# A decoder layer on one core: where ScalarE's tables are loaded, two norms on GpSimd, and another order

## The chip, the cores and the metric

The kernel runs on one core of a Trainium2 chip. The metric is the device time of one execution in microseconds. A core has five engines that run their own instruction streams and meet at semaphores: TensorE (PE in the profile; PEld is its weight load), VectorE (DVE), ScalarE (ACT), GpSimd (POOL) and SyncE (SP), which here only issues DMAs. Products land in PSUM, which TensorE writes and VectorE and ScalarE read; GpSimd works on SBUF alone.

## What is computed

One post-norm decoder layer in float32, for x of shape (4, 1024, 256) and a context of shape (4, 77, 256):

```python
# block 1: sigmoid attention within the rows
q, k, v = x @ Wq.T + bq, x @ Wk.T + bk, x @ Wv.T + bv
qn, kn = layer_norm(q), layer_norm(k)                 # over the 256 columns
attn = sigmoid(qn @ kn.T / sqrt(256) - log(1024))
x = layernorm(x + (attn @ v @ Wo.T + bo) * layerscale)          # the first norm
# block 2: softmax attention over the 77 context rows, 16 heads of 16
qh, kh, vh = heads(x @ wq.T + bq), heads(ctx @ wk.T + bk), heads(ctx @ wv.T + bv)
x = layernorm(x + merge(softmax(qh @ kh.T / 4) @ vh) @ dense.T + b)   # the second norm
# block 3: a channel mix with the row before (zero ahead of row 0)
xr, xk = mu_r * x + (1 - mu_r) * x_prev, mu_k * x + (1 - mu_k) * x_prev
r, kk = sigmoid(xr @ W_r.T), square(relu(xk @ W_k.T))
x = layernorm(x + r * (kk @ W_v.T))                             # the third norm
```

Every norm is (x - mean) / sqrt(var + 1e-5) over the columns.

## The kernel before

The 4096 rows are 32 tiles of 128 rows, taken as 16 pairs (`NJ`). Four pairs are one batch. Products run as three float32r products of a high and a low part each (`split_product`, line 281); so each factor is first copied rounded by ScalarE (`..._hi`, the `copy` of line 460) and its rest taken by VectorE or GpSimd (`..._lo`, line 1170 on VectorE).

Block 1, for pair i: `qk` (query and key product) and their norms, `tqk` (transposes), `v`, then four `scores(4i..4i+3)`, each a 128x512 bank `st` that ScalarE turns into `a_sb` by `sigmoid` (line 510) and copies by `sigmoid_hi`, and four `attend` into the bank `acc`. `attended` and `stats1` on VectorE, `deviation1` on GpSimd (lines 908 to 913, scale `rsl` and bias `nbl`), and `norm1` on ScalarE, which writes x*rsl + nbl back into the rows `xs`.

Block 2: `x1` (transposes of the normed rows, line 1739), `query`, and for each tile t `cross_scores` (line 1886) into four banks `xb`, `maxima` on VectorE (line 1275, four groups of heads, each releases one group of exponentials), `exponentials(t, n)` on ScalarE (line 550, four groups of four 128x77 ACTIVATEs), `fold_weights` (line 948) and `normalise` (line 953) on GpSimd with `sums` and `reciprocals` on VectorE between them, `weights_t` (transposes, line 1899), `mixed` (line 1915), `dense`, and the second norm, on ScalarE for the first seven pairs and on GpSimd after them (line 972, x*rs + nb). The transposes use the same four banks as the logits, so `x1(i)` waits for all exponentials of tile 2i-1, `weights_t(t)` for those of tile t+1, and `cross_scores(t)` for those of tile t-1 and for the copies of the transposes of tile t-2.

Block 3: `x2` (transposes), `carried` (ScalarE, line 460), `halo` (GpSimd, line 984), `mixes` (VectorE, line 1340), `mix_hi`, `mix_lo`, `receptance`, `mix_keys`, `mix_values`, `gate_sigmoid`, `key_relu`, `key_squares`, `gated` (VectorE, line 1364, writes `y`), `residual3` (GpSimd, line 990, adds the rows), `stats3` (VectorE), `deviation3` (GpSimd, lines 997 to 1005) and `norm3`: pairs 0 to 10 on GpSimd (line 1011), 11 to 14 on ScalarE, 15 on VectorE.

Each engine's order is written out by hand: a list of calls for the start, a loop `round_(r)` of calls `at(call, index, count, first)` for the middle, a list for the late part, and `mix_round(i)` and a list for the tail. An engine works strictly in that order. Waits are `w.wait_ge(*sem)`; one that an earlier wait of the engine already covers is left out. ScalarE holds one set of function tables at a time; Sigmoid and Exp are in different sets, while Identity, Relu and Square don't make it load. Nobody writes the loads: where the next ACTIVATE needs the other set, the program gets an ACT_TABLE_LOAD in front of it. If that ACTIVATE has one wait, the wait stays on the ACTIVATE; if it has two, one of them stands on the load.

## Time and profile before

| | us |
|---|---|
| median of 3 runs | 562.71 |
| lowest, highest | 561.57, 563.49 |
| the profiled execution | 561.43 |
| its span | 559.6 |

The span begins with the first instruction on an engine and ends with the last; 1.8 us of the execution lie around it. Roughly, the start lasts until 85 us, the middle rounds until 336 us, the late part of blocks 1 and 2 (no projections left, block 3 beginning from 409 us) until 476 us, and the tail is block 3 alone. The rest is read as follows. A busy share says how much of a stretch an engine spent on instructions, waiting not included. The waits name for each engine which engine's instruction ended an idle time last. The chain goes back from the last instruction to what released it, and so on, so that only its parts set the end.

### The profile page before, as it was taken

What the parts mean: (1) busy time and instruction counts of PE and PEld (TensorE: products, weight loads), DVE (VectorE), ACT (ScalarE), POOL (GpSimd) and SP (SyncE); (2) the same over time, 40 slices, a digit from 0 to 9 for tenths busy, and PEclk for the clock granted to TensorE, in tenths of its full rate; (3) what the DMA queues carried; (4) which work ended last, traced back from release to release, by engine and by line L of the source; (5) the groups of instructions that cost most, each with busy time, mean ns of one, the idle gap of its engine ahead of it and who ended that gap; (6) DMA issues with size and microseconds to landing.
All of it is one profiled execution on the core that took longest, in us unless ns stands there. A gap on an engine that the chain in (4) does not pass through costs nothing.

```text
span 559.6 us, 12593 instructions
## 1 busy us (share of the span) xinstructions
PE 517.6 (92%) x4526; PEld 469.0 (84%) x4526; DVE 450.5 (80%) x1000; ACT 453.9 (81%) x1081; POOL 386.8 (69%) x514
## 2 busy tenths in 40 slices
PE   6989999999999999999999999998996968999873
PEld 4878988898989898998989898877885757999873
DVE  4677859779888788888888887677877998989975
ACT  3672569889899999998899899978897879878854
POOL 2773556766685959586868668466754567799996
PEclk9999999999999999999999999999999999999998
DMA  6511021010001011010101011214100000011113
GB/s 177 164 45 57 2 57 43 2 39 1 2 2 57 1 57 32 27 57 2 58 1 39 2 39 39 68 30 149 41 8 32 1 1 1 20 40 39 57 45 107
DMA packets 24400, 23.01 MB, mean 41 GB/s; under 512 B 2346, under 2 KB 24338, under 8 KB 24338
## 3 DMA queue, kind: packets, MB, share of 16 engines
q1 hardware_dynamic: 24050, 21.94, 12.9%
q8 instruction: 36, 0.59, 0.5%
q10 hardware_dynamic: 288, 0.26, 0.2%
q14 instruction: 26, 0.21, 0.1%
HBM read 15.07 MB, written 6.82 MB: 39 GB/s over the span
## 4 chain that ended last, share of the span: by engine, by line
PE 60%; ACT 14%; DVE 12%; POOL 8%; issue 4%; DMA 1%; POOLq 0%; SPq 0%; DVEq 0%; ACTq 0%
PE st L281 14%; PE acc L281 12%; PE proj L281 9%; PE xb L281 8%; ACT p_sb L550 6%; PE xb L1899 5%; PE xb L1915 4%; PE xb L1886 4%; POOL y L1011 3%; ACT L550 3%; DVE xm L1340 3%; DVE xmT_lo L1170 2%; PE proj L1797 2%; POOL y L990 2%; PE xb L1739 1%
## 5 line engine op out<-in xcount | busy, mean ns | idle before, releaser
L550 ACT ACTIVATE p_sb<-xb,neg_mx 128x77 f32<-128x77 f32 x512 | 118.6, 375 | 1.3 <-DVE neg_mx L1275 1.0
L953 POOL TENSOR_TENSOR p_sb<-p_sb,rc 128x1280 f32<-128x1280 f32 x32 | 78.2, 2443 | 38.6 <-DVE rc L1288 38.6
L948 POOL TENSOR_TENSOR fold<-p_sb 128x640 f32<-128x640 f32 x32 | 50.8, 1587 | 46.6 <-ACT p_sb L550 46.6
L281 PE MATMUL st<-qkT_hi 128*128 128x256 f32 x256 | 76.8, 300 | 0.0
L281 PE MATMUL acc<-vv_hi,aT_hi 128*128 128x256 f32 x256 | 75.5, 295 | 0.5 <-DVE aT_lo L1170 0.5
L281 PE MATMUL st<-qkT_lo,qkT_hi 128*128 128x256 f32 x256 | 72.4, 283 | 0.0
L281 PE MATMUL acc<-vv_hi,aT_lo 128*128 128x256 f32 x256 | 72.3, 283 | 0.0
L281 PE MATMUL acc<-vv_lo,aT_hi 128*128 128x256 f32 x256 | 72.3, 282 | 0.0
L281 PE MATMUL st<-qkT_hi,qkT_lo 128*128 128x256 f32 x256 | 72.3, 282 | 0.0
L1275 DVE TENSOR_REDUCE neg_mx<-xb 128x4 f32<-128x308 f32 x128 | 54.8, 468 | 13.9 <-PE xb L1886 13.6
L1295 DVE COPY pT<-xb 128x512 f32<-128x512 f32 x64 | 43.8, 685 | 19.6 <-PE xb L1899 19.0
L510 ACT ACTIVATE a_sb<-st,nlogs 128x512 f32<-128x512 f32 x64 | 44.0, 689 | 16.6 <-PE st L281 12.0
L281 PEld LDWEIGHTS st<-qkT_hi 128*128 128x128 f32 x256 | 48.7, 190 | 9.1 <-issue 8.6
L1899 PE MATMUL xb<-ident,p_sb 128*128 128x128 f32 x320 | 49.2, 275 | 7.5 <-ACT p_sb L550 6.3
L281 PEld LDWEIGHTS acc<-vv_hi,aT_hi 128*128 128x128 f32 x256 | 48.9, 191 | 1.4 <-DVE aT_lo L1170 0.9
L1170 DVE TENSOR_TENSOR aT_lo<-a_sb,aT_hi 128x512 fp32r<-128x512 f32 x64 | 48.5, 761 | 1.2 <-ACT aT_hi L460 1.2
L897 POOL TENSOR_TENSOR vv_lo<-v_sb,vv_hi 128x512 fp32r<-128x512 f32 x16 | 20.6, 1289 | 41.3 <-ACT vv_hi L460 41.3
L281 PEld LDWEIGHTS st<-qkT_lo,qkT_hi 128*128 128x128 f32 x256 | 48.9, 191 | 0.1
L281 PEld LDWEIGHTS acc<-vv_lo,aT_hi 128*128 128x128 f32 x256 | 48.9, 191 | 0.1
L550 ACT ACT_TABLE_LOAD x30 | 38.5, 1283 | 12.9 <-DVE neg_mx L1275 12.5
L281 PEld LDWEIGHTS st<-qkT_hi,qkT_lo 128*128 128x128 f32 x256 | 48.9, 191 | 0.0
L281 PEld LDWEIGHTS acc<-vv_hi,aT_lo 128*128 128x128 f32 x256 | 48.8, 191 | 0.0
(232 smaller groups left out, 1764.5 us busy)
## 6 DMA issues: line engine op xcount, KB each, us to landing
xraw<-in_xT SPq DMA_DIRECT2D x16, 256.0 KB, 2.9
xs<-in_x SPq DMA_DIRECT2D x16, 256.0 KB, 2.7
out_y<-y SPq DMA_DIRECT2D x16, 256.0 KB, 2.1
x_kept<-xs SPq DMA_DIRECT2D x10, 256.0 KB, 2.1
x2s_a<-x_kept SPq DMA_DIRECT2D x2, 512.0 KB, 5.3
x2s_b<-x_kept SPq DMA_DIRECT2D x2, 512.0 KB, 7.8
x2s_c<-x_kept SPq DMA_DIRECT2D x1, 512.0 KB, 3.6
cT<-in_cT SPq DMA_DIRECT2D x1, 308.0 KB, 3.1
```

The costliest lines, as they stand in the source:

```text
L281: mm = pe.matmul(out, s_, m_, start=first and k == 0 and q == 0, stop=last and k == n - 1 and q == 2, skip_group_check=not check)
L510: act.activation(a_sb[:, i % NAR], st_bank[i % 2], ACT.Sigmoid, bias=nlogs[:, 0:1], scale=1.0 / 16).then_inc(sg_act.sem, 1)
L550: ex = act.activation(weights(t)[:, h // KH * (H // 2) + KH * n + h % KH, 0:SC], logits[n][:, h * SC:(h + 1) * SC], ACT.Exp, bias=neg_mx[: ...
L897: pool.tensor_tensor(lo, tiles(v_sb[:]), f(hi), ALU.subtract).then_inc(v_pool.sem, 1)
L948: pool.tensor_tensor(fold[:].rearrange("p (h k) -> p h k", k=FO), p[:, :, 0:FO], p[:, :, FO:2 * FO], ALU.add).then_inc(fo_pool.sem, 1)
L953: pool.tensor_tensor(weights(t), weights(t), rc[:, t % 2].rearrange("p (h o) -> p h o", o=1) .to_broadcast([P, H, SP]), ALU.mult).then_inc ...
L1170: return dve.tensor_tensor(lo, whole, f(hi), ALU.subtract)
L1275: dve.tensor_reduce(neg_mx[:, t % 2, HG * n:HG * (n + 1)], logits[n][:, 0:HG * SC].rearrange("p (h k) -> p h k", k=SC), AX, ALU.min)\
L1295: dve.tensor_copy(pT[:, 4 * c:4 * c + 4, (t % 2) * P:(t % 2 + 1) * P], tiles(tp_bank(c), 4))\
L1886: mm = pe.matmul(logits[n][:, e * KW:(e + 1) * KW], xq[own, e * D + u * P:e * D + (u + 1) * P], kb[own, b, e], start=True, stop=True)
L1899: mm = pe.transpose(tp_bank(c)[:, (n - 4 * c) * P:(n - 4 * c + 1) * P], p_sb[:, t % NP, n * P:(n + 1) * P], ident[:])
L1915: mm = pe.matmul(pv_bank[32 * n:32 * (n + 1), k * D:(k + 1) * D], vb[:, n, half, :, :, KC * b + k].rearrange("p a d -> p (a d)"), pT[:, 5 ...
```

## The change

ScalarE: `table_for(func)` is called at the head of `sigmoid`, `exponentials` and `gate_sigmoid`. Where the function differs from that of the call before, it issues an ACTIVATE of `func` on one column (`nlogs`, 128x1) into a column of `spare` that nobody reads, and the table load goes in front of that one. There are 61 such ACTIVATEs, and 62 loads before and after.

GpSimd: the first norm of pairs 11 to 15 (`N1 = 11`) is done there as multiply and add; `x1` and `deviation1` wait for the engine that does it. The third norm of pairs 0 to 10, still on GpSimd, becomes x*rs3 + nb3 in place of (x - mean)*rs3; so `nb3` is computed for all pairs but the last, and `stats3` waits for `nb3` of the pair two before it instead of for its norm.

The order of all engines is written anew. The rounds on ScalarE and TensorE start one pair later with more written out ahead of them; what a round does is the same but for its order.

```diff
+N1 = 11
+NSPARE = 8
...
+        def self_norm(i):
+            return ln1_act.at(i) if i < N1 else ln1_pool.at(i - N1)
...
+                loaded, spares = [None], count()
+                def table_for(func):
+                    if loaded[0] != func:
+                        loaded[0] = func
+                        w.wait_ge(*consts_pool.at(0))
+                        n = 8 * (next(spares) % NSPARE)
+                        act.activation(spare[:, n:n + 1], nlogs[:], func)
                 def sigmoid(i):
+                    table_for(ACT.Sigmoid)
                     w.wait_ge(*st_pe.at(i))
...
                 def exponentials(t, n):
+                    table_for(ACT.Exp)
                     w.wait_ge(*pads_pool.at(0))
...
                 def gate_sigmoid(i):
+                    table_for(ACT.Sigmoid)
                     w.wait_ge(*fr_pe.at(i))
...
                 def round_(r):
-                    at(exponentials, 2 * r - 6, NT, 2, 2)
-                    at(tqk_hi, 2 * r + 5, NT, 13)
+                    at(xt_hi, r + 3, NJ, 9)
+                    at(weights_tail, 2 * r - 9, NTA, 3)
...
                 def deviation1(i):
                     w.wait_ge(*ln1s_dve.at(i))
                     if i:
-                        w.wait_ge(*ln1_act.at(i - 1))
+                        w.wait_ge(*self_norm(i - 1))
...
+                def norm1(i):
+                    w.wait_ge(*ln1n_pool.at(i))
+                    for t in range(2):
+                        x1 = rows_of(i)[:, t]
+                        pool.tensor_scalar(x1, x1, rsl[:, t:t + 1], nbl[:, t:t + 1], ALU.mult, ALU.add).then_inc(ln1_pool.sem, 1)
...
                 def deviation3(i):
                     w.wait_ge(*fvs_dve.at(i))
                     if i - 2 >= NJ - NL:
                         w.wait_ge(*ln3_act.at(i - 2 - (NJ - NL)))
+                    elif i >= 2:
+                        w.wait_ge(*ln3_pool.at(i - 2))
...
-                    if NJ - NL <= i < NJ - 1:
-                        n, nb = i - (NJ - NL), nb3[:, i % 2]
+                    if i < NJ - 1:
+                        nb = nb3[:, i % 2]
...
                 def norm3(i):
-                    w.wait_ge(*ln3s_pool.at(i))
+                    w.wait_ge(*ln3n_pool.at(i))
                     for t in range(2):
                         yt = y[:, i % NY, t]
-                        pool.tensor_scalar(yt, yt, mv3[:, i % 2, t, 0:1], rs3[:, i % 2, t:t + 1],
-                                           ALU.subtract, ALU.mult).then_inc(ln3_pool.sem, 1)
+                        pool.tensor_scalar(yt, yt, rs3[:, i % 2, t:t + 1], nb3[:, i % 2, t:t + 1],
+                                           ALU.mult, ALU.add).then_inc(ln3_pool.sem, 1)
...
                 def stats3(i):
-                    if i - 2 >= NJ - NL:
-                        w.wait_ge(*ln3n_pool.at(i - 2 - (NJ - NL)))
-                    elif i >= 2:
-                        w.wait_ge(*ln3_pool.at(i - 2))
+                    if i >= 2:
+                        w.wait_ge(*ln3n_pool.at(i - 2))
...
                 def x1(i):
-                    w.wait_ge(*ln1_act.at(i))
+                    w.wait_ge(*self_norm(i))
```

How the order moves at the places that matter later. First ScalarE in late attention, from the sigmoid ahead of the exponentials of tile 27 to the transposed rows of pair 14. `p_sb<-xb` is an exponential, `a_sb<-st` a sigmoid, `xs<-xs,nbl,rsl` the first norm, `x1T_hi` the copy of the transposed rows. Before:

```order
L510 ACTIVATE a_sb<-st,nlogs 128x512 [waits s_st_dve,s_st_pe]
L550 ACT_TABLE_LOAD [waits s_mx_dve]
L550 ACTIVATE p_sb<-xb,neg_mx 128x77 [waits s_tp_pe]
L550 ACTIVATE p_sb<-xb,neg_mx 128x77 x3
...
L460 ACTIVATE xs<-xs,nbl,rsl 128x256 [waits s_ln1n_pool]
L460 ACTIVATE xs<-xs,nbl,rsl 128x256
L460 ACTIVATE aT_hi<-a_sb 128x512 [waits s_av_pe,s_sg_act]
L460 ACTIVATE x1T_hi<-xb 128x512 [waits s_tx_pe]
```

And now the same tile and pair:

```order
L521 ACT_TABLE_LOAD
L521 ACTIVATE spare<-nlogs 128x1
L570 ACTIVATE p_sb<-xb,neg_mx 128x77 [waits s_mx_dve,s_tp_pe]
L570 ACTIVATE p_sb<-xb,neg_mx 128x77 x3
...
L521 ACT_TABLE_LOAD
L521 ACTIVATE spare<-nlogs 128x1
L529 ACTIVATE a_sb<-st,nlogs 128x512 [waits s_st_dve,s_st_pe]
L468 ACTIVATE x1T_hi<-xb 128x512 [waits s_tx_pe]
```

The wait for the maxima (`s_mx_dve`) has left the load, the first norm has left ScalarE, and a sigmoid with its load stands ahead of the transposed rows.

Second GpSimd, in the tail, around the last residual add with the second batch's rows (`x2s_b`) and the first with the third's (`x2s_c`); `rs3` and `nb3` are scale and bias of the third norm, `y` its rows. Before:

```order
L1011 TENSOR_SCALAR y<-y,mv3,rs3 128x256
L990 TENSOR_TENSOR y<-y,x2s_b 128x512 [waits s_fva_dve]
L997 TENSOR_TENSOR rs3<-mv3,consts 128x2 [waits s_fvs_dve]
L999 TENSOR_TENSOR rs3<-rs3,consts 128x2 [waits s_ln3s_pool]
L984 COPY carry<-carry 128x4 [waits s_ca_act,s_xm_dve]
L990 TENSOR_TENSOR y<-y,x2s_c 128x512 [waits s_fva_dve]
```

And now:

```order
L1067 TENSOR_TENSOR rs3<-mv3,consts 128x2 [waits s_ln3_pool,s_fvs_dve]
L1069 TENSOR_TENSOR rs3<-rs3,consts 128x2 [waits s_ln3s_pool]
L1072 TENSOR_TENSOR nb3<-mv3,consts 128x2
L1075 TENSOR_TENSOR nb3<-nb3,rs3 128x2 [waits s_ln3n_pool,s_ln3s_pool]
L1058 TENSOR_TENSOR y<-y,x2s_b 128x512 [waits s_fva_dve]
L1052 COPY carry<-carry 128x4 [waits s_ca_act,s_xm_dve]
L1058 TENSOR_TENSOR y<-y,x2s_c 128x512 [waits s_fva_dve]
L1081 TENSOR_SCALAR y<-y,rs3,nb3 128x256 [waits s_ln3n_pool]
L1081 TENSOR_SCALAR y<-y,rs3,nb3 128x256
```

Each pair has two small instructions more, and the norm reads `rs3` and `nb3` in place of `mv3` and `rs3`.

## Rows read from the trace of the kernel before

**Rows 1.** The page: busy us and shares; TensorE's busy tenths in 40 slices

```profile
PE 517.6 (92%) x4526; PEld 469.0 (84%) x4526; DVE 450.5 (80%) x1000; ACT 453.9 (81%) x1081; POOL 386.8 (69%) x514
...
PE   6989999999999999999999999998996968999873
```

**Rows 2.** Stretches: length, busy us and instructions of each engine, clock, DMA share, GB/s

```profile
200.00:226.07 26.07, 26.07 (x242) 23.90 (x241) 21.91 (x50) 23.69 (x60) 18.99 (x25) 1.00 0.11 32
...
336.00:434.00 98.00, 88.51 (x834) 78.00 (x833) 72.14 (x149) 83.19 (x213) 60.72 (x67) 1.00 0.17 52
434.00:476.00 42.00, 33.99 (x326) 29.15 (x325) 38.67 (x84) 36.95 (x103) 27.39 (x35) 1.00 0.01 1
490.00:546.00 56.00, 48.98 (x396) 47.16 (x394) 49.27 (x117) 42.80 (x90) 54.90 (x66) 1.00 0.14 48
```

**Rows 3.** TensorE in order of time: start us, us, what; one middle round

```profile
199.93 0.28 PE L281 MATMUL xb<-x1T_hi,wx_hi 128*128 128x256 f32 x1
...
209.57 0.47 PE L281 MATMUL proj<-wqk_hi,xT_hi 128*128 128x512 f32 x1
209.88 0.40 PE L281 MATMUL proj<-wqk_lo,xT_hi 128*128 128x512 f32 x1
210.11 0.39 PE L281 MATMUL proj<-wqk_hi,xT_lo 128*128 128x512 f32 x1
...
226.00 0.28 PE L281 MATMUL xb<-x1T_hi,wx_hi 128*128 128x256 f32 x1
```

**Rows 4.** Waits, 336:476 and 476:560: who for whom, us, times, longest

```profile
ACT L550 <- DVE neg_mx L1275: 10.6, 8, 3.3
...
DVE st L1374 <- POOL y L990: 6.0, 6, 1.4
```

**Rows 5.** Groups of ScalarE, whole span: busy us, mean ns, idle before

```profile
L550 ACT ACTIVATE p_sb<-xb,neg_mx 128x77 f32<-128x77 f32 x512 | 118.6, 375 | 1.3 <-DVE neg_mx L1275 1.0
...
L550 ACT ACT_TABLE_LOAD x30 | 38.5, 1283 | 12.9 <-DVE neg_mx L1275 12.5
L510 ACT ACT_TABLE_LOAD x29 | 37.2, 1283 | 0.5
```

**Rows 6.** ScalarE in order of time; in brackets idle before, and releaser

```profile
76.12 1.28 ACT L550 ACT_TABLE_LOAD   x1 [1.92 <-DVE neg_mx L1275]
...
405.71 1.28 ACT L550 ACT_TABLE_LOAD   x1 [0.85 <-DVE neg_mx L1275]
...
407.01 3.57 ACT L550 ACTIVATE p_sb<-xb,neg_mx 128x77 f32<-128x77 f32 x16
...
430.73 1.28 ACT L550 ACT_TABLE_LOAD   x1 [3.33 <-DVE neg_mx L1275]
```

**Rows 7.** The chain that ended last: start us, us, what; tile 27, pair 14

```profile
416.82 1.28 ACT L550
...
421.68 0.98 ACT xs L460 x2
...
422.71 0.67 PE xb L1739 x4
```

**Rows 8.** GpSimd in order of time: start us, us, what

```profile
418.09 0.20 POOL L913 TENSOR_TENSOR nbl<-nbl,rsl 128x2 f32<-128x2 f32 x1
...
504.44 1.10 POOL L972 TENSOR_SCALAR xs<-xs,rs,nb 128x256 f32<-128x256 f32 x2
505.52 2.43 POOL L1011 TENSOR_SCALAR y<-y,mv,rs 128x256 f32<-128x256 f32 x2
```

**Rows 9.** Groups of GpSimd, whole span: busy us, mean ns, idle before

```profile
L1011 POOL TENSOR_SCALAR y<-y,mv,rs 128x256 f32<-128x256 f32 x22 | 28.3, 1294 | 0.2
...
L972 POOL TENSOR_SCALAR xs<-xs,rs,nb 128x256 f32<-128x256 f32 x18 | 12.6, 709 | 0.1
...
L1002 POOL TENSOR_TENSOR nb<-mv,consts 128x2 f32<-128x2 f32 x4 | 0.9, 232 | 0.0
L1005 POOL TENSOR_TENSOR nb<-nb,rs 128x2 f32<-128x2 f32 x4 | 0.8, 198 | 0.6
```

More of the change, by code:

```diff
@@ L1 @@
 from contextlib import ExitStack
+from itertools import count
 import numpy as np
@@ new lines, in round_ @@
+                    at(weights_tail, 2 * r - 9, NTA, 3)
+                    at(sigmoid, 4 * r - 7, NS, 16)
+                    at(mixed_hi, r - 5, NJ, 1)
+                    at(sigmoid, 4 * r - 6, NS, 16)
+                    at(exponentials, 2 * r - 7, NT, 4, 0)
+                    at(exponentials, 2 * r - 7, NT, 4, 1)
+                    at(exponentials, 2 * r - 7, NT, 4, 2)
+                    at(sigmoid_hi, 4 * r - 7, NS, 16)
+                    at(exponentials, 2 * r - 7, NT, 4, 3)
@@ new lines, in round_ @@
+                    at(norm1, r - 3, N1, 3)
+                    at(sigmoid_hi, 4 * r - 6, NS, 16)
+                    at(tqk_hi, 2 * r + 4, NT, 15)
+                    at(x1_hi, r - 3, NJ, 3)
+                    at(sigmoid, 4 * r - 5, NS, 16)
+                    at(v_hi, r + 2, NJ, 7)
+                    at(norm2, r - 6, N2)
+                    at(weights_tail, 2 * r - 8, NTA, 3)
+                    at(sigmoid, 4 * r - 4, NS, 16)
+                    at(query, r - 3, NJ, 2)
+                    at(sigmoid_hi, 4 * r - 5, NS, 16)
@@ L733, in _ @@
                 weights_tail(0)
+                query(1)
+                sigmoid(12)
+                exponentials(2, 0)
+                exponentials(2, 1)
                 sigmoid_hi(11)
+                exponentials(2, 2)
+                tqk_hi(13)
+                exponentials(2, 3)
+                weights_tail(1)
+                sigmoid(13)
+                sigmoid_hi(12)
+                mixed_hi(0)
+                sigmoid(14)
+                exponentials(3, 0)
+                exponentials(3, 1)
+                exponentials(3, 2)
+                exponentials(3, 3)
+                sigmoid_hi(13)
+                norm1(2)
+                xt_hi(8)
+                tqk_hi(14)
+                sigmoid_hi(14)
+                x1_hi(2)
+                sigmoid(15)
+                sigmoid_hi(15)
+                weights_tail(2)
                 for r in range(NJ):
                     round_(r)
+                sigmoid(57)
+                mixed_hi(11)
+                sigmoid_hi(57)
+                exponentials(25, 0)
+                exponentials(25, 1)
+                exponentials(25, 2)
+                exponentials(25, 3)
+                sigmoid(58)
+                x1_hi(13)
+                sigmoid_hi(58)
+                sigmoid(59)
+                sigmoid(60)
+                query(13)
+                exponentials(26, 0)
+                sigmoid_hi(59)
+                exponentials(26, 1)
+                sigmoid_hi(60)
                 exponentials(26, 2)
                 exponentials(26, 3)
-                carried(0)
                 sigmoid(61)
@@ L742, in _ @@
                 sigmoid_hi(61)
-                sigmoid(62)
                 exponentials(27, 0)
@@ L747, in _ @@
                 exponentials(27, 3)
-                norm1(14)
+                sigmoid(62)
+                x1_hi(14)
                 sigmoid_hi(62)
-                x1_hi(14)
+                carried(0)
                 sigmoid(63)
+                query(14)
                 sigmoid_hi(63)
-                query(14)
                 exponentials(28, 0)
@@ L1575, in _ @@
                 maxima(4, 2)
+                sigmoid_lo(15)
+                sigmoid_lo(16)
+                weights_body(3, 0)
                 for r in range(NJ):
```

649 lines of the change are left out of this document (333 added, 316 removed).

## Prediction

> **What bounds the kernel now.** I read the busy shares first, then the same shares by stretch, then in each stretch the wait that ends last. The page says TensorE 92%, ScalarE and VectorE 80 to 81%, GpSimd 69% [rows 1]. The 40 slices of 14 us show that these shares are an average over stretches that differ: TensorE has a 9 in every slice from 42 to 378 us, 6 to 9 in the seven after them, and 8, 7 and 3 in the last three [rows 1].
>
> *Middle rounds.* One whole round (a pair of row tiles) takes 26.07 us: the query product starts at 199.93 and again at 226.00 [rows 3]. In it TensorE is busy for all of the 26.07 us with 242 matmuls, ScalarE for 23.69, GpSimd for 18.99 [rows 2]. Nothing that shortens ScalarE or GpSimd shortens such a round. ScalarE has 2.38 us of idle time in it.
>
> *Late attention, 336 to 434 us.* No projections are left to fill TensorE: it is busy for 88.51 of 98 us, and its weight loads for 78.00, where the share of the middle rounds (23.90 of 26.07) would give 89.8 [rows 2]. So 9.5 to 12 us of TensorE's time are lost here. The chain of waits says to whom: maxima on VectorE, a table load of 1.28 us on ScalarE, 16 exponentials, the first norm (0.98 us), and only then TensorE's transposes [rows 7]. The row of waits says that ScalarE sat idle 10.6 us in 8 places before a table load of the exponentials [rows 4].
>
> *Tail, 490 to 546 us.* Only the third block is left. GpSimd is busy 54.90 of 56 us, VectorE 49.27, TensorE 48.98, ScalarE 42.80 [rows 2]. VectorE waited 6.0 us of it for GpSimd's residual add [rows 4]. GpSimd bounds this stretch, with VectorE 6.7 us behind.
>
> **The change, part by part.**
>
> *Table loads ahead of waits.* The number of loads stays 62. In the order of before, the first exponential of a tile from 20 on has two waits, and the one on the maxima stands on the load; in the changed order it stands on the exponential, with a 128x1 ACTIVATE between. Sigmoid loads gain nothing: all 29 together waited 0.5 us [rows 5]. Exponential loads of the middle rounds did not wait either; their 12.9 us of idle time is in nine places [rows 5], eight of them in late attention. There the load can now run inside the idle time, so each place gains the smaller of its wait and 1.28 us, less what the ACTIVATE adds where the wait is short. The eight waits sum to 10.6 us [rows 4]; the longest, 3.33 [rows 6], is cut to 1.28, which leaves 8.5.
>
> Price of the new ACTIVATE: no row shows a 128x1 on ScalarE. The nearest is the 128x77 exponential: 16 take 3.57 us, 223 ns apart [rows 6]. Not below nothing, since it does the engine no service; not above 375 ns, the mean of a 77-column one by itself [rows 5]. I take 0.17 us, below the spacing because it has 76 columns less. The seven shorter waits are about as long as the load or shorter, so 7 x 0.17 = 1.2 is lost there: 8.5 - 1.2 = 7.3 us, between 5.9 (at 0.375 us) and 8.5. All eight places are on the chain, as [rows 7] shows for one. In the middle rounds four of them cost 0.7 us (1.5 at most) and lie in ScalarE's 2.38 us of idle time; without that cover they would cost their full price on each of some ten rounds.
>
> The skill (Trainium skill, "ScalarE: Activation LUTs", section "What ACT_TABLE_LOAD costs") puts a switch at 1283 ns plus a drain of about 1380. The load agrees; the drain does not show, as the exponentials at 407.01 begin 1.30 us after the start of their load [rows 6]. With a drain on each of the eight places the gain by that page would be up to twice as large where the wait is long enough; I leave it out.
>
> *First norm of pairs 11 to 15 on GpSimd.* ScalarE loses ten ACTIVATEs, GpSimd gains ten instructions of the shape of its second norm, 0.55 us each when undisturbed (1.10 for two), 0.71 in the mean [rows 8, 9]. On the chain the ScalarE norm of pair 14 starts at 421.68, after the exponentials, though GpSimd had its numbers at 418.29 [rows 7, 8]. GpSimd would be done by 419.4, before the exponentials end, so 0.98 us leaves the chain. The same stands at pairs 12 and 13 (374.24 and 397.91, not repeated): 3 x 0.98 = 2.9 us. But the new order puts a sigmoid and its load where the norm was (1.28 + 0.17 + 0.69 = 2.1 us), ahead of the copy of the transposed rows, which before began 1.7 us after the exponentials; so that copy comes 0.4 us later and all behind the two of them 1.0 us earlier. I take 2.0 us, between -1 and 4. What is queued behind it on GpSimd is the second norm's numbers and the next fold; GpSimd is busy 60.72 of 98 us here [rows 2], which covers 5.5 to 7.1 us more.
>
> *Sum for late attention.* 7.3 + 2.0 = 9.3 us, against 9.5 to 12 us that TensorE loses there. A chain hardly gives back all of its length, because the next one (VectorE's, seen as the wait of 3.33 us, which is VectorE working through its own queue) is close behind. I take three quarters: -7.0, between -3 and -10.
>
> *Third norm as multiply and add.* GpSimd's (y - mean) x rs takes 1294 ns per tile, its x rs + nb of the same shape 709 [rows 9]; undisturbed neighbours in the tail are 1.10 us for two at 504.44 and 2.43 for two at 505.52 [rows 8]. 22 tiles x 0.585 = 12.9 us saved. Eleven more pairs need nb, 0.232 + 0.198 us each [rows 9] = 4.7 us. Net -8.2 us of GpSimd, on the engine that bounds the tail. But VectorE comes next after 6.7 us, and ScalarE's and TensorE's queues are near too. I take -5, between -2 and -7. The last few us behind the last product keep their length: pairs 11 to 14 stay normed on ScalarE and 15 on VectorE.
>
> Here a page speaks against the change. By the Trainium skill, "GPSIMD Engine Reference", section 3.1, GpSimd's time goes by the number of tensor inputs, two being the dear case. Both forms have one, so by that page only the 4.7 us of nb would be left and the edit would cost time. Rows decide: at the same shape, in the same stretch, 1.10 against 2.43.
>
> *New order.* On TensorE a middle round has the same 242 matmuls, but four runs of transposes instead of three. A product that follows such a run starts its second matmul after 0.31 us instead of 0.23 [rows 3], so about 0.1 us per round: +1.0 over ten rounds. For the explicit part I have no price, only that neighbours are exchanged and nothing moves by more than a few places: 0, between -3 and +3. Start: the first exponential load sat behind 1.92 us of waiting at 76.12 [rows 6] on the chain; -1.28 and three ACTIVATEs of 0.17 us, about -0.8, between 0 and -2.
>
> **Sum.** -7.0 - 5 + 1.0 - 0.8 = -11.8 us. The profiled execution took 561.43 us (span 559.6), so 549.6. The median of the runs shown is 1.28 us higher, so I forecast 550.9 us.
>
> **The rivals.**
>
> *A. The gains are eaten.* VectorE is busy 38.67 of 42 us in 434 to 476 [rows 2], the stretch that takes over what late attention gives back. If what late attention saves waits again there and VectorE takes half of the tail's gain, -3.5 - 2.5 + 1 - 0.8 = -5.8: 557 us. For it: the wait of 3.33 us. Against it: VectorE's 72.14 of 98 us before that.
>
> *B. Slower: ScalarE becomes the bound of the middle rounds.* Place: the four loads of a round, each with an ACTIVATE more. It decides from the point where the ACTIVATE costs over 0.6 us (2.38 / 4), or where the new order leaves ScalarE's idle time in places that it cannot use, so that each round grows by the full four. Price at 0.375 us: 1.5 us x 10 rounds = +15, with -11.8 for the rest: +3.2, 566 us. Against it: 91% busy with idle time spread over four waits in a round.
>
> *C. The form doesn't matter.* If GpSimd's norm was slow for its place and not for its operations, the saturated tail gets 4.7 us longer: -7.0 + 4.7 + 1.0 - 0.8 = -2.1, 560.6 us. Against it stands the pair of rows above.
>
> *D. More than the sum.* The chain gives back all (-9.3), the tail its 6.7, the order another 3, the start 0.8: -19.8, 543 us.
>
> **How the numbers follow.** Forecast (545 to 554) 0.55; A 0.20; B 0.08; C 0.04; D 0.08; 0.05 for something unseen, half of it on either side. The range reaches from D's edge to just beyond A: 543 to 560. A measurement of this kernel can tell about 0.3%, 1.7 us. Faster: forecast, A, D and most of C and the unseen, 0.87; same 0.04; slower 0.09.
>
> **What would show it.** Table loads before exponentials with no wait on maxima, and waits on the exponential itself; the first norm of pairs 12 to 14 gone from the chain; the third norm on GpSimd near 0.6 to 0.7 us; GpSimd under 90% from 490 us on with VectorE above; a middle round of 26.1 to 26.2 us. A round above 26.5 us is B; a third norm of 1.2 us is C; late attention as long as before with other waits is A.

## The result, and the profile after

The changed kernel takes 540.09 us in the median (539.50 to 540.18), the kernel before, beside it on the same chip, 562.14 (561.37 to 563.49). The ratio is 0.9603, with a 95% interval of 0.9581 to 0.9625: 22.05 us less, where 11.8 less were forecast and 543 was the low end of the range. The direction was right, the size was not. In the profiled executions the span went from 559.6 to 538.4 us, 21.2 less.

The page of the changed kernel answers [rows 1]: busy us, share, instructions, and TensorE's and VectorE's busy tenths in 40 slices.

```profile
PE 513.4 (95%) x4526; PEld 467.9 (87%) x4526; DVE 448.4 (83%) x1000; ACT 452.9 (84%) x1132; POOL 374.1 (69%) x546
...
PE   6999999999999999999999999999999987999994
...
DVE  4786878888888888887979797778878989999995
```

TensorE now has a 9 in every slice from 13 to 525 us but two, which lie from 431 to 458 us. The stretches of [rows 2], a round of 25.97 us first:

```profile
199.70:225.67 25.97, 25.97 (x243) 23.81 (x242) 22.10 (x50) 23.88 (x63) 17.80 (x24) 1.00 0.11 32
336.00:434.00 98.00, 94.46 (x925) 84.39 (x924) 79.43 (x175) 87.62 (x245) 69.93 (x83) 1.00 0.16 51
434.00:476.00 42.00, 37.51 (x347) 33.24 (x348) 40.07 (x90) 39.28 (x98) 32.29 (x48) 1.00 0.03 9
490.00:546.00 56.00, 40.48 (x332) 39.60 (x331) 41.52 (x105) 38.07 (x79) 40.29 (x74) 0.95 0.17 58
```

In late attention TensorE works 94.46 us of 98, against 88.51. In the middle rounds it is full, as before. In the tail GpSimd is busy for 40.29 us behind 490, less than VectorE's 41.52, as the prediction's sign had it; the kernel ends at 538.4.

The groups by line answer [rows 5, 9]: busy us, mean ns, idle before.

```profile
L521 ACT ACT_TABLE_LOAD x61 | 78.3, 1283 | 1.1
L1081 POOL TENSOR_SCALAR y<-y,rs,nb 128x256 f32<-128x256 f32 x22 | 13.4, 620 | 0.1
L521 ACT ACTIVATE spare<-nlogs 128x1 f32<-128x1 f32 x61 | 12.4, 203 | 0.7
L1040 POOL TENSOR_SCALAR xs<-xs,rs,nb 128x256 f32<-128x256 f32 x18 | 11.9, 671 | 0.1
L1075 POOL TENSOR_TENSOR nb<-nb,rs 128x2 f32<-128x2 f32 x15 | 4.8, 323 | 2.1
L1072 POOL TENSOR_TENSOR nb<-mv,consts 128x2 f32<-128x2 f32 x15 | 4.1, 272 | 0.0
```

The loads hardly wait any more (1.1 us before all 61), the 128x1 ACTIVATE takes 0.203 us (0.17 was the estimate), and the third norm on GpSimd takes 620 ns where it took 1294. The waits of 330 to 440 us, for [rows 4]:

```profile
ACT p_sb L570 <- DVE neg_mx L1359: 2.0, 5, 0.8
```

And the chain that ended last, at tile 25, for [rows 7] (start us, us, what):

```profile
387.20 0.49 DVE neg_mx L1359
...
387.77 1.98 ACT p_sb L570 x9
389.75 0.10 issue
389.85 1.48 ACT p_sb L570 x6
391.33 0.02 issue
391.35 1.28 ACT L521
...
392.75 0.68 ACT a_sb L529
```

From the maxima the chain goes straight to the exponentials, with no load and no norm between; behind them it now holds a sigmoid with its load.

**Where the time went.** ScalarE's copy of the mixed values of a pair (`oT_hi`) is a mark that every kernel has. Its starts for pairs 8 and 13 in the changed kernel:

```profile
316.55 0.60 ACT L468 ACTIVATE oT_hi<-xb 128x512 fp32r<-128x512 f32 x1 [0.82 <-PE xb L2000]
...
427.31 0.60 ACT L468 ACTIVATE oT_hi<-xb 128x512 fp32r<-128x512 f32 x1 [1.77 <-PE xb L2000]
```

The same mark, read from each trace, cuts each kernel into stages (us). "Pair 13 to end" uses the span. Each row is one trace, and each median is over all executions of the kernel. The experiments are explained below.

| kernel | pair 0 at | 0 to 8 | 8 to 13 | 13 to end | median us |
|---|---|---|---|---|---|
| before | 108.66 | 208.76 | 120.97 | 121.21 | 562.14 |
| changed | 108.82 | 207.73 | 110.76 | 111.09 | 540.09 |
| b_table | 109.37 | 209.40 | 114.85 | 119.78 | 554.16 |
| b_norm3 | 109.08 | 208.69 | 122.29 | 116.14 | 557.38 |
| b_norm1 | 107.86 | 208.73 | 117.87 | 121.54 | 558.15 |
| b_all3 | 107.23 | 209.50 | 111.90 | 115.47 | 545.43 |
| a_none | 108.95 | 207.85 | 123.79 | 118.81 | 560.39 |
| a_untable | 108.58 | 207.84 | 121.88 | 113.40 | 552.63 |
| a_unnorm3 | 108.21 | 207.76 | 110.87 | 117.46 | 545.75 |
| a_unnorm1 | 108.08 | 207.76 | 114.25 | 112.61 | 544.73 |
| a_3spare | 108.52 | 208.81 | 111.69 | 111.48 | 542.15 |
| all3_lo14 | 108.60 | 209.58 | 111.93 | 116.19 | 547.11 |
| all3_fill | 107.99 | 209.53 | 111.94 | 113.84 | 545.36 |
| all3_two | 107.58 | 209.52 | 111.84 | 112.46 | 543.72 |
| a_swap | 108.16 | 207.76 | 110.83 | 112.25 | 541.05 |
| a_exponly | 108.21 | 207.84 | 110.63 | 111.12 | 539.57 |
| a_best1 | 108.32 | 207.85 | 110.71 | 110.42 | 539.49 |
| a_best2 | 108.69 | 207.84 | 110.66 | 111.51 | 540.49 |
| after_again (the changed kernel) | 107.71 | 207.76 | 110.84 | 112.59 | 539.91 |
| a_best1_again | 109.73 | 207.83 | 110.64 | 110.30 | 538.70 |

How far can one trace be trusted? Pair 0 comes anywhere between 107.2 and 109.7 us, also among kernels whose start is the same; so differences of a microsecond there say nothing. The rounds repeat within some 0.1 us where nothing was changed. The other two stages don't always:

- *The clock.* b_norm3 and the kernel before run the same instructions until 477 us, and the marks of pairs 8 and 12 lie 96.4 and 96.5 us apart. From 429 to 435 us TensorE is busy for 3.3 of 6 us in both. In b_norm3 its granted clock then falls (0.84, then 0.59, in the stretches of 3 us from 432), in the trace of before it stays at 1.00, and 8 to 13 takes 122.29 against 120.97 us. So this stage scatters by 1.3 us in kernels with such gaps.
- *The end.* The two traces of the changed kernel agree in the rounds and in late attention, and from pair 13 to pair 15 as well (43.15 and 43.22 us), but pair 13 to end is 111.09 in one and 112.59 in the other. A difference below 1.5 us in the last column of stages therefore says little; where one matters, the text gives 13 to 15.

The clock also parts medians from stages. Of the 38 executions of the kernel before that were measured beside the experiments, two had a mean clock of 0.995 (560.03 and 561.25 us) and 36 had 0.985 to 0.992 (561.19 to 565.71 us); the trace of before is of an execution at 0.995. All eight of the changed kernel had 0.995 to 0.998. So before's stages in the table hold none of the clock that its median has lost, and the medians show larger gains than the stages do.

### The profile page after: what moved, and what is told of

Read it like the earlier page. It is cut to its first block, busy times and chain, and to the rows that moved or that the text cites. A ratio compares the mean times of both kernels' runs of the same rounds, so it can differ in the third digit from the quotient of the medians.

```text
span 538.4 us, 12700 instructions
## 1 busy us (share of the span) xinstructions
PE 513.4 (95%) x4526; PEld 467.9 (87%) x4526; DVE 448.4 (83%) x1000; ACT 452.9 (84%) x1132; POOL 374.1 (69%) x546
## 4 chain that ended last, share of the span: by engine, by line
PE 71%; ACT 12%; DVE 9%; issue 3%; POOL 1%; DMA 1%; SPq 0%; POOLq 0%; DVEq 0%; ACTq 0%
PE st L285 16%; PE acc L285 16%; PE xb L285 11%; PE proj L285 9%; PE xb L2000 5%; PE xb L1984 5%; ACT p_sb L570 5%; PE xb L1971 4%; ACT L521 2%; PE proj L1882 2%; DVE xm L1424 2%; PE xb L1824 1%; DMA bqk<-in_bk 1%; DVE xmT_lo L1254 1%; ACT carry L468 1%
## 5 line engine op out<-in xcount | busy, mean ns | idle before, releaser
L1021 POOL TENSOR_TENSOR p_sb<-p_sb,rc 128x1280 f32<-128x1280 f32 x32 | 74.9, 2341 | 25.6 <-DVE rc L1372 25.6
L285 PE MATMUL st<-qkT_hi 128*128 128x256 f32 x256 | 74.8, 292 | 0.2 <-ACT a_sb L529 0.2
L468 ACT ACTIVATE aT_hi<-a_sb 128x512 fp32r<-128x512 f32 x64 | 43.3, 679 | 0.1
```

Source lines behind the costliest of these rows:

```text
L285: mm = pe.matmul(out, s_, m_, start=first and k == 0 and q == 0, stop=last and k == n - 1 and q == 2, skip_group_check=not check)
L468: return act.activation(out, in_, ACT.Identity, **kw)
L1021: pool.tensor_tensor(weights(t), weights(t), rc[:, t % 2].rearrange("p (h o) -> p h o", o=1) .to_broadcast([P, H, SP]), ALU.mult).then_inc ...
```

## The experiments

### The three edits, each alone in the order of before, and together

b_table has `table_for` alone:

```diff
+                def table_for(func): ...
                 def sigmoid(i):
+                    table_for(ACT.Sigmoid)
                 def exponentials(t, n):
+                    table_for(ACT.Exp)
                 def gate_sigmoid(i):
+                    table_for(ACT.Sigmoid)
```

> The kernel before, in its own order, with the first edit alone: a 128x1 ACTIVATE of the next function ahead of the waits. Theory (the edits bring their gains by themselves, in either order): the eight places of late attention shrink by 7 to 8 us and 5 to 7 us of it reach the end: 555 to 557 us, with the waits of VectorE's reductions now standing on the exponential and no longer on the table load. Rival (the new order brings the gain, and the edits only fit it): -3 us or less, 559 to 562 us, because the next chain is as long. The middle rounds stay within 0.1 us of 26.07 us by both: the ACTIVATEs (0.20 us each in the trace of the changed kernel) lie in ScalarE's idle time.

554.16 us, ratio 0.9835 (0.9808 to 0.9862). The theory, and more than it: the median is 9.0 us lower. The stages show -6.1 us in late attention, -1.4 behind pair 13 (-1.2 up to pair 15) and +0.6 in the rounds, 6.9 in all.

b_norm3 has the third norm and its `nb3` alone, with the waits of `deviation3` and `stats3` as in the change:

```diff
-                    if NJ - NL <= i < NJ - 1:
+                    if i < NJ - 1:
...
-                        pool.tensor_scalar(yt, yt, mv3[:, i % 2, t, 0:1], rs3[:, i % 2, t:t + 1],
-                                           ALU.subtract, ALU.mult).then_inc(ln3_pool.sem, 1)
+                        pool.tensor_scalar(yt, yt, rs3[:, i % 2, t:t + 1], nb3[:, i % 2, t:t + 1],
+                                           ALU.mult, ALU.add).then_inc(ln3_pool.sem, 1)
```

> The kernel before with the third norm of pairs 0 to 10 as multiply and add on GpSimd, and nothing else. Theory (GpSimd bounds the tail, and its time counts there until VectorE comes next): GpSimd's instruction falls from 1.29 us to about 0.62, the end comes 5 to 7 us earlier, 555 to 557 us; all of it behind 434 us, and nothing ahead of that moves. Rival (the tail's gain of 10 us in the changed kernel came from its order): -3 us or less, 559 to 562 us, with VectorE then waiting for its own queue or for TensorE.

557.38 us, ratio 0.9891 (0.9856 to 0.9925). Behind pair 13 it is 5.1 us shorter, as forecast. The stage ahead of it is 1.3 us longer by the fall of the clock told above, which isn't the edit's doing: its first instruction runs at 477 us.

b_norm1 has the first norm of pairs 11 to 15 on GpSimd, right behind its `deviation1` (here in its loop):

```diff
                     at(deviation1, r - 2, NJ, 1)
+                    at(norm1, r - 2, NJ, N1)
```

> The kernel before with the first norm of pairs 11 to 15 on GpSimd, right behind its own numbers, and nothing else. Theory: ScalarE's norm (0.98 us for a pair) leaves the chain at three to five pairs, -2 to -4 us, 558 to 560 us. Rival (the copy of the transposed rows goes on as late, or GpSimd's slower instruction, 0.58 us against ScalarE's 0.49, takes the norm's place on the chain): within 1 us of the kernel before, 561 to 563 us.

558.15 us, ratio 0.9911 (0.9883 to 0.9938). Late attention is 3.1 us shorter, about the 0.98 us of each of three pairs.

b_all3 is before's order with all three.

> The kernel before, in its own order of instructions, with all three edits: what this one leaves to the changed kernel (540.1 us) is what the new order brings. Theory (the edits bring most): 543 to 549 us, the order 3 to 9 us. Rival (the order brings at least half): 551 us or more. A second question is whether the three single edits add up: their sum against this one.

545.43 us, ratio 0.9679 (0.9656 to 0.9702). In late attention 9.1 us are gone, and 6.1 + 3.1 = 9.2: the two edits add up in full. Behind pair 13 it is 5.7. By the medians the edits bring 17 to 18 us, and the new order 5.3 more (4.3 by the ratios to the kernel before, which is the fairer figure for two different chips, and good for about 2 us either way). By the stages the order brings 1.8 us in the rounds, 1.1 in late attention and 4.4 behind pair 13 (2.9 against the changed kernel's second trace).

### The other way round, in the new order

a_none has none of the edits, a_untable, a_unnorm3 and a_unnorm1 lack one each: the diffs above undone, and for a_unnorm1 and a_none

```diff
-N1 = 11
+N1 = 16
...
                 exponentials(25, 3)
+                norm1(13)
...
                 exponentials(27, 3)
+                norm1(14)
...
                 mixed_hi(13)
+                norm1(15)
```

> The changed kernel's order with none of the three edits: table loads behind their waits, the third norm as subtract and multiply, the first norm of all pairs on ScalarE. Theory (edits and order are separate, the order brings about 5 us in either): 556 to 559 us. Rival (the order is made for the edits and is worth nothing, or costs, without them): 561 us or more.

560.39 us, ratio 0.9961 (0.9945 to 0.9976), 2.4 us below the kernel before: between the theory and the rival.

> The changed kernel without the ACTIVATEs ahead of the table loads. In the order of before this edit alone was worth 9.0 us, and the order without any edit 2.4. Theory (the new order lets TensorE's gaps in late attention be filled by other means, so the edits overlap little with it): 547 to 550 us, 7 to 10 us above the changed kernel, all of it between 330 and 470 us. Rival (with the order written for them the edits are worth more than alone): 551 us or more.

552.63 us: 12.5 above the changed kernel. Here the rival was right. By the stages the edit is worth 11.1 us in late attention, where it was worth 6.1 in the order of before.

> The changed kernel with the old third norm on GpSimd (subtract and multiply, no nb for pairs 0 to 10). Alone in the order of before the edit was worth 5.7 us. Theory (GpSimd's time is what the tail pays for until VectorE comes next): 546 to 548 us, nothing changed ahead of 450 us. Rival (the new tail gave GpSimd more room): 541 to 544 us.

545.75 us: 5.7 above. By the stages it is 6.4 behind pair 13, or 4.9 against the changed kernel's second trace. The theory, a little under its range.

> The changed kernel with the first norm of pairs 11 to 15 on ScalarE again, behind the exponentials of tiles 2i-1 as in the order of before. Alone in the order of before the edit was worth 3 to 5 us. Theory (0.98 us on the chain for each of pairs 11 to 14): 543 to 545 us. Rival (the new order has put other work in that place and the norm fits beside it): at most 1.5 us, 540 to 541.6.

544.73 us: 4.6 above, 3.5 in late attention and 1.5 between pairs 13 and 15. The theory.

Without the edits the new order is worth 2.4 us, with them 4.3 to 5.3; these two medians alone don't part clearly. The stages do: without the table edit late attention takes 121.88 or 123.79 us in the new order, no less than the 120.97 to 122.29 of the old one, and with it 110.76 against 111.90. The order fits the edits there. Part of it is TensorE's clock, which falls at two places of this stage in a_none and a_untable. The second in a_untable, 431 to 437 us (columns as in [rows 2]):

```profile
431.00:437.00 6.00, 5.18 (x38) 4.36 (x42) 4.76 (x7) 4.16 (x17) 3.14 (x5) 0.72 0.00 0
```

At 0.72 some 1.7 us of TensorE's 6 are lost (an estimate, 0.28 x 6); the stretch ahead of it, 428 to 431 us, had TensorE busy for 1.73 us of 3.

### What the ACTIVATE costs

```diff
                         act.activation(spare[:, n:n + 1], nlogs[:], func)
+                        for _ in range(2):
+                            n = 8 * (next(spares) % NSPARE)
+                            act.activation(spare[:, n:n + 1], nlogs[:], func)
```

> The changed kernel with three 128x1 ACTIVATEs in place of one at each of the 61 table loads: it measures what such an ACTIVATE costs and how near ScalarE is to bounding the middle rounds. Alone one takes 0.20 us by the trace, two in a row should be spaced by 0.10 to 0.20. A middle round has four loads and ScalarE 2.0 us of idle time in 25.97 us. Theory (idle time covers them): the rounds stay within 0.3 us of 25.97 and only some 8 to 12 places of late attention pay 0.2 to 0.4 us each, 542 to 545 us in all. Rival (ScalarE's idle time lies where it can't be used): each of ten rounds grows by 0.8 to 1.6 us, 548 to 556 us.

542.15 us. Two more ACTIVATEs at 61 loads cost 2.1 us: 1.1 over the eight rounds of 0 to 8 (0.13 a round), 0.9 in late attention, and 0.4 behind it, which is within the scatter. Rival B of the prediction, ScalarE as the bound of the middle rounds, is refuted even at three times the ACTIVATEs.

In the old order, though, the one ACTIVATE did cost 0.07 us a round. TensorE's round shows one place of it, alike in all eight rounds. Start of the last two transposes of a tile and of the product behind them, in before, b_table and the changed kernel:

```profile
235.41 0.38 PE L1899 MATMUL xb<-ident,p_sb 128*128 128x128 f32 x2
235.63 0.47 PE L281 MATMUL proj<-wqk_hi,xT_hi 128*128 128x512 f32 x1
```

```profile
236.47 0.38 PE L1914 MATMUL xb<-ident,p_sb 128*128 128x128 f32 x2
236.78 0.47 PE L283 MATMUL proj<-wqk_hi,xT_hi 128*128 128x512 f32 x1
```

```profile
234.93 0.38 PE L1984 MATMUL xb<-ident,p_sb 128*128 128x128 f32 x2
235.07 0.48 PE L285 MATMUL proj<-wqk_hi,xT_hi 128*128 128x512 f32 x1
```

The product comes 0.22 us behind them in before, 0.31 in b_table and 0.14 in the changed kernel; it is 0.14 in a_none too, so it is the order that does it and not an edit. A TensorE that is 100% busy by the windows can still hold small waits, and the new order took this one away.

### What the new order does behind pair 13

b_all3 and the changed kernel differ in their order alone, and 4.4 of the difference lie behind pair 13, 3.8 of it between pairs 13 and 15. The trace of b_all3 shows a gap on TensorE and its clock behind it; the same stretches in all3_fill stand under it:

```profile
447.00:450.00 3.00, 0.17 (x8) 0.07 (x4) 3.00 (x7) 1.98 (x5) 1.61 (x3) 0.87 0.00 0
450.00:456.00 6.00, 6.00 (x38) 5.69 (x39) 4.25 (x10) 5.38 (x20) 2.68 (x2) 0.50 0.01 3
```

```profile
447.00:450.00 3.00, 3.00 (x37) 2.55 (x30) 3.00 (x6) 2.08 (x5) 2.42 (x3) 1.00 0.00 0
450.00:456.00 6.00, 5.09 (x51) 4.51 (x50) 5.96 (x13) 5.91 (x21) 2.48 (x2) 1.00 0.01 3
```

In b_all3 TensorE idles and then runs 38 matmuls in 6 us at 0.50 (1.2 GHz); with the gap filled it runs 51 in 5.09 us at 1.00.

```diff
                 mixed(14)
+                w.wait_ge(*fr_act.at(0))
+                for n in range(18):
+                    pe.matmul(st_bank[0][:, 0:D], w_f[0][:, MIX_R, 0, 0:P], w_f[0][:, MIX_R, 0], start=True, stop=True)
                 cross_scores(31)
```

> The kernel before with all three edits, its order unchanged, and 18 products without use (128x128 by 256 columns, into a free bank) on TensorE ahead of the cross scores of tile 31, in the gap of 2.83 us. It takes away the idle time and nothing of the wait. Theory (idle TensorE loses its clock, and that costs the time): clock at 1.00 through the stretch, 2 to 4 us less than 545.4. Rival (the gap's wait itself is what costs, and the clock costs nothing): 545 to 546 us, with the clock at 1.00.

545.36 us, no different from b_all3 in the median. By its stages it is 1.6 us shorter behind pair 13, all of it between pairs 13 and 15, which its later pair 0 (107.99 against 107.23) half hides. The cross scores behind the products start 2.75 us after pair 14's mark, as they did without them (2.77), so the fill changed little but the clock. In these two traces it costs about 1.6 us, less than the theory said. In the median no gain was shown: the trace of b_all3 is of its slowest execution, and the four with the fill range from 544.62 us at a mean clock of 0.996 to 547.29 at 0.989, so the clock falls in some of them all the same.

```diff
+                mixed_lo(14)
                 mix_lo(1)
                 mixes(2)
-                mixed_lo(14)
```

> The kernel before with all three edits (545.4 us, span 544.1) and one exchange in its order: VectorE takes the low part of pair 14's mixed rows ahead of the low parts and mixes of the third block that stood before it. In the trace of the kernel with the three edits those two hold VectorE for 4.2 us while TensorE waits (2.83 us idle from 447.1), and right behind that gap the granted clock of TensorE stands at 0.50 for some 7 us, which the changed kernel does not show. Theory (part of what the new order brings in the tail is that TensorE keeps its clock): the gap is gone, the clock stays at 1.00, and the time falls by 2 to 4 us, to 541.5 to 543.5. Rival (the clock dip lies where VectorE or ScalarE bound the kernel anyway): at most 1 us less, 544.5 to 546, clock dip or not.

547.11 us: slower by 1.7, which neither theory nor rival expected. The low part did start 0.63 us behind pair 14's mark instead of 1.95, but VectorE had waited 2.76 us for it, and the mixes and low parts now behind it came later: the first `gated` is 6.1 us behind the mark instead of 5.4, and from 448 to 462 us the clock stood at 0.76 in both.

What held VectorE at this place is a collision. In order of time (start us, us, what), b_all3 on VectorE and then on GpSimd, and under it the changed kernel in the same way:

```profile
444.98 2.67 DVE L1200 TENSOR_TENSOR xmT_lo<-xm,xmT_hi 128x512 fp32r<-128x512 f32 x2
447.57 1.65 DVE L1370 SCALAR_TENSOR_TENSOR xm<-proj,mu,carry 128x256 f32<-128x256 f32 x4
449.14 0.67 DVE L1200 TENSOR_TENSOR oT_lo<-xb,oT_hi 128x512 fp32r<-128x512 f32 x1
...
445.11 1.99 POOL L973 TENSOR_TENSOR fold<-p_sb 128x640 f32<-128x640 f32 x1 [0.33 <-ACT p_sb L570]
```

```profile
443.53 1.65 DVE L1424 SCALAR_TENSOR_TENSOR xm<-proj,mu,carry 128x256 f32<-128x256 f32 x4
445.10 1.28 DVE L1254 TENSOR_TENSOR xmT_lo<-xm,xmT_hi 128x512 fp32r<-128x512 f32 x2
446.37 0.69 DVE L1254 TENSOR_TENSOR oT_lo<-xb,oT_hi 128x512 fp32r<-128x512 f32 x1
...
443.65 1.55 POOL L1016 TENSOR_TENSOR fold<-p_sb 128x640 f32<-128x640 f32 x1 [0.82 <-ACT p_sb L570]
```

`mix_lo` subtracts two SBUF operands. Beside GpSimd's `fold`, its two instructions take 2.67 us and the fold 1.99; apart they take 1.28 and 1.55. `mixes`, whose one operand is in PSUM, takes 1.65 beside the fold and the fold its 1.55. In the changed kernel the subtractions overlap GpSimd's second norm instead; they keep their 1.28 us, and the norm takes 1.52 us for two instructions where 1.09 is usual. This agrees with the Trainium skill, "SBUF — State Buffer", section "Who interferes with whom": a VectorE instruction with two SBUF inputs contends with a GpSimd instruction that reads SBUF, since the second input comes through the interface that both share.

The trace of before has the same collision, and the same idle time of TensorE behind it (2.83 us from 456.8):

```profile
454.67 2.66 DVE L1170 TENSOR_TENSOR xmT_lo<-xm,xmT_hi 128x512 fp32r<-128x512 f32 x2
...
454.79 1.99 POOL L948 TENSOR_TENSOR fold<-p_sb 128x640 f32<-128x640 f32 x1 [0.32 <-ACT p_sb L550]
```

The changed kernel has the two neighbours the other way round. all3_two gives b_all3 this exchange and one at the end:

```diff
-                mix_lo(1)
                 mixes(2)
+                mix_lo(1)
                 mixed_lo(14)
...
+                stats3(14)
                 gated(15)
                 residual3(15)
-                stats3(14)
```

> The kernel before with all three edits (545.4 us) and two exchanges of neighbours on VectorE, both of which the changed kernel has. First, the mixes of pair 2 ahead of the low part of pair 1's mixes: with the old order that low part, a subtraction of two SBUF operands, took 2.67 us for two instructions where 1.28 is usual, beside a two-input add of GpSimd, and what follows on TensorE came 1.3 us later than in the changed kernel. Second, the last but one third-block statistics ahead of the last gated product. Theory (what the order brings in the tail are such single places: a collision of VectorE with GpSimd, TensorE's clock behind the gap, one misplaced neighbour at the end): 1.3 us at the first place, up to 1.6 us more if the clock then stays at 1.00, 1.0 us at the second: 541.5 to 543 us. Rival (the gain of the order is spread over the tail): 544 to 545.5 us.

543.72 us, 1.7 below b_all3, and 3.0 less behind pair 13, 2.8 of it up to pair 15. The two low parts take 1.29 us, and the clock stays at 1.00 from 448 to 462 us. The second exchange gave next to nothing: from `gated` of pair 14 to the end it is 10.0 us against 10.2. And the reverse, in the changed kernel:

```diff
+                mix_lo(1)
                 mixes(2)
-                mix_lo(1)
                 mixed_lo(14)
```

> The changed kernel with the first of these two exchanges undone: on VectorE the low part of pair 1's mixes ahead of the mixes of pair 2. Theory (the collision with GpSimd's fold costs VectorE 1.4 us at this place, and TensorE's wait behind it may cost the clock too): the low part takes 2.0 us instead of 0.68, 541.3 to 543 us. Rival (the phase of GpSimd is another one here, or the delay is absorbed): 540 us, as the changed kernel.

541.05 us, 1.0 above: its four executions took 540.85 to 541.28 us, the changed kernel's eight 539.05 to 540.71. The collision is back (VectorE, then GpSimd):

```profile
442.99 2.67 DVE L1254 TENSOR_TENSOR xmT_lo<-xm,xmT_hi 128x512 fp32r<-128x512 f32 x2
...
443.11 1.99 POOL L1016 TENSOR_TENSOR fold<-p_sb 128x640 f32<-128x640 f32 x1 [0.84 <-ACT p_sb L570]
```

From pair 13 to 15 it is 1.2 us longer (44.36 against 43.15 and 43.22), about the 1.4 by which the two subtractions grew. The rest of the order's gain behind pair 13, 112.46 - 111.09 = 1.4 us, has no single place that these runs show, and is no more than the changed kernel's two traces differ by there.

That scatter has a cause that can be seen. In the second trace the two subtractions of `mix_lo` at 509.98 us take 2.38 us, beside GpSimd's residual add of 1.67; in the first the add starts at 511.59 and they take 1.28. In the second trace TensorE then idles 1.07 us up to 515.5 for VectorE's next low part. The same kernel meets this collision in one execution and not in the next.

### Can the changed kernel be bettered?

a_exponly leaves the ACTIVATEs ahead of the sigmoids' loads out:

```diff
                 def sigmoid(i):
-                    table_for(ACT.Sigmoid)
+                    loaded[0] = ACT.Sigmoid
```

> The changed kernel with the ACTIVATE ahead of the waits for the 32 exponential loads alone; the 29 loads for the sigmoid stand behind their waits as before. Two more ACTIVATEs at each load cost 2.1 us in all, so one costs about 1, and half of them are at sigmoids. Theory (the sigmoids' loads never waited, so their ACTIVATEs are only a cost): 539.3 to 540 us, up to 0.7 us less. Rival (in the tail, where ScalarE waits for TensorE's receptance products, the load ahead of the wait helps): 540.5 to 543 us.

539.57 us (539.47 to 539.73) on another chip: the theory by its number, and no more than a hint. a_best1 and a_best2 also take away a collision of `mix_lo(4)` with the residual add at 464.5 us:

```diff
+                mix_lo(4)
                 gated(1)
-                mix_lo(4)
                 mixes(5)
```

> The changed kernel with the ACTIVATE ahead of exponential loads only (539.57 us) and VectorE's low part of pair 4's mixes ahead of the gated product of pair 1. There the same subtraction takes 1.78 us instead of 0.68, since GpSimd's residual add starts when the gated product is done; VectorE is busy without a break in this stretch. Theory (a microsecond of VectorE here is one of the kernel): 538.3 to 539 us. Rival (TensorE or the later gated product takes its place): 539.3 to 540.5 us.

539.49 us. The subtractions take 1.28 us instead of 2.38, and behind pair 13 it is 0.7 us shorter than a_exponly; the median doesn't show it.

> The same aim in another way: behind the gated product of pair 1 come the mixes of pair 5, which read PSUM, and only then the low part of pair 4's mixes. Theory: 538.3 to 539 us if the products of pair 4, now 1.6 us less the 1.1 saved later, don't hold TensorE; rival: they do, 539.6 to 540.5 us.

540.49 us: the rival's number, but not its reason. The subtractions are quick again (1.28 us), but VectorE waits 1.32 us ahead of the mixes of pair 5, for ScalarE's `carry`, which is about as long as the collision was.

> The changed kernel once more, five rounds, on the same chip as the next one, so that the two can be compared directly. 540.1 us by the first measurement, 539.5 to 540.5 expected, with the clock at 0.995 or above in every run.

539.91 us (539.05 to 540.71), with the clock at 0.995 or 0.996 in all four runs, as expected.

> The changed kernel with the ACTIVATE ahead of exponential loads only and VectorE's low part of pair 4 ahead of the gated product of pair 1, once more, five rounds beside the changed kernel. Theory (the collision taken away and 29 ACTIVATEs fewer are worth 0.6 us together, as the stages of the traces say): 0.4 to 0.8 us below the changed kernel in the same call. Rival (only the different chips made it look so): within 0.3 us of it.

538.70 us (538.08 to 540.33) beside these, ratios to the kernel before of 0.9571 (0.9545 to 0.9597) and 0.9593 (0.9567 to 0.9620). Both times the version was ahead, by 0.6 and 1.2 us; the intervals overlap, so it is likely the faster one and not shown to be. The 1.2 us are more than the theory's 0.4 to 0.8.

## Why the prediction was wrong, step by step

| term | forecast | stages, changed against before |
|---|---|---|
| late attention (8 to 13) | -7.0 | -10.2 |
| tail (13 to end) | -5 | -10.1 (-8.6 by the second trace) |
| middle rounds (0 to 8) | +0.8 of +1.0 | -1.0 |
| start | -0.8 | +0.2 (within its scatter) |

**The bound was read rightly.** Each stage's reading held: rounds that ScalarE can't lengthen (a_3spare), eight places of late attention where a load stood between maxima and exponentials (b_table), a tail that pays for GpSimd (b_norm3, a_unnorm3). Rivals B and C are refuted; A too: between pairs 13 and 15 nothing was waited for again (46.4 us before, 43.2 in the changed kernel). D, "more than the sum", was nearest: it had late attention at -9.3 and a better order. One number of the tail was read wrongly: VectorE stood 54.90 - 49.27 = 5.6 us behind GpSimd, and the 6.7 is its idle time in 56 us.

**Failed step 1: three quarters.** I summed 9.3 us for the table loads and the first norm and then took three quarters because "a chain hardly gives back all of its length". The two edits in the old order brought 9.1 of the 9.3. The single terms were off in opposite directions, 6.1 for 7.3 and 3.1 for 2.0. The discount had no row behind it; the 9.5 to 12 us that TensorE was seen to lose there spoke against it. Of the norm's term I had taken off 0.9 us for the sigmoid put in its place; undoing the norm in the new order costs 3.5 us in this stage, so the deduction was wrong as well.

**Failed step 2: the explicit order at 0.** It was called neighbours exchanged with no price. It brings 1.1 us in late attention and 4.4 behind pair 13: 3.0 at one place, where one exchange takes a VectorE subtraction out from beside GpSimd's fold and TensorE then keeps its clock, and 1.4 that may be scatter. A good part of this price stood in the trace of before: 2.66 us at 454.67 for two subtractions that take 1.28 elsewhere, on the way to 2.83 us of idle TensorE, just where the new order exchanges neighbours. That the exchange alone, without the edits, would give it back was not run. A range of 3 either way for "order" was also too narrow for a kernel whose every stage was reordered.

**Failed step 3: the sign in the rounds.** The one more run of transposes is there. But a round became 0.10 us shorter, and 0.08 of it is the small wait shown above, which windows and waits had not shown.

**Failed step 4: the clock carried over.** The forecast adds 1.28 us because the median of before lay above its profiled execution. The changed kernel's median lies 0.06 us below its own (540.09 and 540.15). No term of the sum was for TensorE's clock, whose mean was below 0.995 in 36 of 38 executions of before and in none of the changed kernel's eight; the two of before that kept it were 0.9 and 3.1 us below the medians beside them.

**Right terms.** The third norm: -5 forecast, 5.1 in the old order, 4.9 or 6.4 in the new. Per instruction it saved more (1294 to 569 ns in b_norm3) and nb cost more (595 ns for the two small instructions in the changed kernel, 430 forecast). The Trainium skill, "GPSIMD Engine Reference", section 3.1, makes two tensor inputs the dear case. Here two forms with one tensor input each differ by a factor of two, so its number doesn't decide alone, and the measurement does. Operations and scalar operands were changed together, and no run parts them. The ACTIVATE: 0.17 forecast, 0.20 measured. Behind pair 13 the table edit gave another 1.4 (old order) to 2.3 us (new), 1.2 and 2.3 of it up to pair 15, which I had not counted: exponentials of the last tiles run there beside block 3. The start can't be judged, as pair 0 scatters by 2 us.

## What to carry to other kernels

Add up what stands on a chain and compare it with what the bounding engine loses in that stretch; when the two agree, take the sum and no discount. Measure an order together with the edits it was written for: the table edit was worth 6.1 us of late attention in one order and 11.1 in the other. On VectorE, put an instruction that reads PSUM, not one with two SBUF inputs, beside a long two-input GpSimd instruction, and look for one subtraction in the trace that takes twice as long as its like. Before you read a microsecond out of one trace, take a second of the same kernel and see which stages repeat.

## What the runs showed of the hardware

- A multiply and add on GpSimd takes 569 to 620 ns in the mean for 128x256 float32 (b_norm3, changed), a subtract and multiply of the same shape 1294 to 1347 (before, a_unnorm3), each with one tensor input and two scalars per partition.
- VectorE's subtraction of two SBUF operands (0.68 us) and GpSimd's adds hold each other up: 2.67 us for two beside a fold of 1.99, 1.28 and 1.55 apart; 2.38 beside a residual add of 1.67.
- TensorE's granted clock stood at 0.50 for 6 us behind a stretch of 3 us in which it was busy for 0.17; filling the gap with products without use kept it at 1.00. It was worth 1.6 us at a place where VectorE and ScalarE were nearly as busy. Behind one and the same gap (TensorE busy for 3.3 of 6 us) the clock fell in one trace and stayed in another.
- A first ACTIVATE of 128x1 behind a load takes 203 ns; two more take 0.28 us together.
